# A decoder's first sublayer: triangular solve by halves of four tiles, two heads per operation

## The chip, the core and the metric

The kernel is one program on one core of a Trainium2 chip. It computes a four-layer decoder forward pass. The metric is the device time of the whole program in microseconds (us), median of several runs. Engines: TensorE (PE in the profile; PEld is its weight load), VectorE (DVE), ScalarE (ACT), GpSimd (POOL), SyncE (SP). PSUM, which PE writes, has eight banks of 512 fp32 columns on 128 partitions.

## What is computed

The change touches the first of eleven sublayers only, a gated delta rule attention with 6 heads, 32 key and 64 value channels, on 16 sequences of 64 tokens:

```
q = silu(conv(x @ Wq.T)); k = silu(conv(x @ Wk.T)); v = silu(conv(x @ Wv.T))
beta = sigmoid(x @ Wb.T);  g = -exp(A_log) * softplus(x @ Wa.T + dt_bias)
q, k = l2norm(q) * DK ** -0.5, l2norm(k)
def step(S, (qt, kt, vt, gt, bt)):          # over the 64 tokens
    S = S * exp(gt)
    v_new = vt - kt @ S
    S = S + bt * outer(kt, v_new)
    return S, qt @ S
o = scan(step); o = rmsnorm(o) * norm_w * silu(x @ Wg.T); x = x + o @ Wo.T
```

## The kernel before

The scan over tokens is written as a linear system for each head and sequence, solved by a blocked inverse. The 1024 tokens are 8 tiles (NT) of 128 partitions, and a tile holds two sequences of 64 (the two `halves` of the partitions, 0 to 63 and 64 to 127). So each step of the solve is, for one head, 8 tiles x 2 halves = 16 products of 64x64 by 64x64, one below the other on the diagonal of the PE array: `tile_position=(SEQ * half, SEQ * half)`, that is (0, 0) and (64, 64) in turn. An fp32 product is two matmul records in the trace, so a step of one head is a group of 32 records of 64 columns. The result of a head fills one PSUM bank, and one DVE or ACT operation of 128x512 takes it out.

The heads go in three pairs (a, b), and the solve stage runs from L2942 to L3353. `Fl` holds the levels of the system, made on POOL by `level` (L3140); `Rm` is the inverse built so far and `Tm` its transpose; `Wm` is a working square. For a pair and each of levels 1 to 4:

- `first` (L3009): PE forms W from `Fl` and `Tm`; ACT copies it out in `copy_w` (L3177);
- `second`: PE forms the update of the transpose (L3022, levels 1 to 3 only) and of the inverse (L3026); DVE subtracts them in `update` (`Tm` at L3254, `Rm` at L3255).

Then `solve` (L3034), copy (L3206), `pulled` (L3044), copy (L3209), `corrected` (L3052), `settled` on DVE (L3262), `outputs` (L3060), copy (L3215), squares (L3219, L3266). Between the groups of a pair PE does the front work for the heads of the next pair, n and m: `decays` (L2966), `keys` and `queries` (both L2974), `turn` (L2996). Its DVE steps are `decayed` (L3228), `pulls` (L3235), `reads` (L3241), `start` (L3245: identity minus level 0, the first inverse) and `copy_turned` (L3249). Each engine's queue is in the order in which it is written, and semaphores join them. `hold` (L1688) is filler work on PE. The stage behind (L3358 on) normalises and projects; its DVE queue begins at L3376.

The lists of buffers before the stage (L2865 to L2927) give each head squares of its own; heads 0 and 1 use banks 0 to 2 and 3 to 5 for the solve, and banks 6 and 7 serve the front work (3 and 4 for head 1).

## Time and profile before

| | us |
|---|---|
| median of 3 runs | 1345.42 (1344.11 to 1345.56) |
| the profiled execution, its own time | 1344.42 |
| span of its trace | 1342.7 |
| share of the span PE / DVE / ACT / POOL busy | 93% / 59% / 44% / 28% |
| mean granted PE clock | 0.993 of 2.4 GHz |

The profile is of one execution. The page gives busy times and groups over the whole program. The changed stage is under a tenth of it (about 84 to 198 us of the trace), so the readings below are from the time lines, windows and waits of that stretch. Matmuls overlap, so that "busy" of PE and the mean of one record say little; what a group costs is the distance from its start to the start of the next.

### The profile page before, as it was taken

Reading aid. Unit: us, or ns where it says so; the run is one execution under the profiler, and the core shown is the slowest. Engines: PE = TensorE matmul, PEld = TensorE weight load, DVE = VectorE, ACT = ScalarE, POOL = GpSimd, SP = SyncE. Lnnn points to the kernel's source line nnn. Section 1 sums busy time; section 2 is a strip of 40 time slices with the busy share of each in tenths; the row PEclk is TensorE's granted clock in tenths of the full one; section 3 lists DMA queues with packets and bytes.
Section 4 is the critical chain, followed back from the end, with each engine's and each line's share of the span. In section 5 each row is a group of like instructions: output and inputs, shape, how many; then the busy total and the mean of one; then the engine's idle time right before and its main releaser. Section 6 shows DMA issues by size and latency. Waiting matters only on the chain. (4 is left out here: it accounts for less than half of the span.)

```text
span 1342.7 us, 30256 instructions
## 1 busy us (share of the span) xinstructions
PE 1245.0 (93%) x12658; PEld 932.8 (69%) x12658; DVE 798.1 (59%) x1511; ACT 591.1 (44%) x1070; POOL 378.9 (28%) x323
## 2 busy tenths in 40 slices
PE   6999998989999999999999889999997888999988
PEld 3479994559977677788867667888774445676545
DVE  5764566863363764633358665888644775873762
ACT  3632334684554674433433431232532453662751
POOL 0164303046630000555520005544102043532100
PEclk9999999999999999999999999999998999999999
DMA  4000004046024001000075080000016421211000
GB/s 125 4 2 4 4 4 127 1 109 131 1 68 146 2 2 36 1 0 1 1 165 166 1 264 1 1 1 2 2 71 199 133 61 47 55 30 33 2 1 32
DMA packets 81047, 68.36 MB, mean 51 GB/s; under 512 B 24968, under 2 KB 76880, under 8 KB 80784
## 3 DMA queue, kind: packets, MB, share of 16 engines
q1 hardware_dynamic: 78096, 63.63, 16.8%
q8 instruction: 101, 1.65, 0.5%
q0 software_dynamic: 768, 2.10, 0.5%
q10 hardware_dynamic: 2048, 0.70, 0.2%
q14 instruction: 34, 0.28, 0.1%
HBM read 53.82 MB, written 8.39 MB: 46 GB/s over the span
## 5 line engine op out<-in xcount | busy, mean ns | idle before, releaser
L1955 PE MATMUL ps<-rounded 128*128 128x512 f32 x384 | 91.2, 393 | 2.0 <-POOL rounded L1988 1.0
L1688 PE MATMUL ps<-fixed 128*128 128x512 bf16 x361 | 89.6, 389 | 1.9 <-PEq L78 1.9
L1342 POOL TENSOR_TENSOR fixed<-fixed,cross 128x768 f32<-128x768 f32 x32 | 58.9, 1839 | 104.5 <-DVE cross L1291 104.5
L1955 PEld LDWEIGHTS ps<-rounded 128*128 128x128 f32 x384 | 70.9, 188 | 20.3 <-POOL rounded L1988 5.3
L1256 PE MATMUL ps<-rounded 128*128 128x256 f32 x576 | 76.8, 287 | 1.3 <-DVE cross L1287 1.3
L1256 PEld LDWEIGHTS ps<-rounded 128*128 128x128 f32 x576 | 70.7, 190 | 5.4 <-issue 3.2
L1988 POOL TENSOR_TENSOR rounded<-weights,rounded 128x256 fp32r<-128x256 f32 x32 | 23.6, 760 | 179.7 <-ACT rounded L2006 179.7
L1321 ACT COPY cross<-ps 128x256 f32<-128x256 f32 x32 | 11.9, 372 | 112.9 <-PE ps L1265 112.9
L1688 PEld LDWEIGHTS ps<-fixed 128*128 128x128 bf16 x361 | 34.7, 99 | 37.8 <-issue 6.9
L2095 DVE TENSOR_TENSOR work<-work,ps 128x512 f32<-128x512 f32 x32 | 22.0, 687 | 62.0 <-ACT work L2023 59.9
L1629 POOL TENSOR_TENSOR work<-weights,work 64x512 f32<-64x512 f32 x32 | 41.2, 1287 | 54.3 <-DMA work<-work 33.5
L1265 PE MATMUL ps<-fixed,work 128*128 128x256 f32 x192 | 49.3, 393 | 7.4 <-POOL fixed L1342 7.0
L1876 DVE SCALAR_TENSOR_TENSOR fixed<-ps,work,fixed 128x256 f32<-128x256 f32 x64 | 27.7, 479 | 46.7 <-PE ps L1779 46.7
L227 PE MATMUL ps<-fixed 128*128 128x128 f32 x160 | 30.3, 303 | 20.8 <-ACT fixed L212 16.2
L525 DVE TENSOR_REDUCE work<-ps 128x16 f32<-128x1024 f32 x32 | 39.2, 1224 | 17.5 <-PE ps L373 16.9
L201 ACT ACTIVATE fixed<-fixed 128x2 f32<-128x2 f32 x48 | 13.6, 293 | 80.7 <-DVE fixed L173 80.6
L1805 POOL TENSOR_TENSOR rounded<-work,rounded 128x512 fp32r<-128x512 f32 x32 | 41.1, 1300 | 27.7 <-ACT rounded L1836 27.2
L1779 PE MATMUL ps<-rounded 128*128 128x256 f32 x384 | 47.9, 284 | 0.0
L1779 PEld LDWEIGHTS ps<-rounded 128*128 128x128 f32 x384 | 47.2, 192 | 1.0 <-POOL rounded L1805 0.4
L1974 PEld LDWEIGHTS ps<-rounded 128*128 128x128 f32 x384 | 47.0, 192 | 0.5
L1974 PE MATMUL ps<-rounded 128*128 128x256 f32 x384 | 47.2, 283 | 0.0
L1752 PE MATMUL ps<-rounded 128*128 128x512 f32 x192 | 45.8, 393 | 1.4 <-POOL rounded L1792 1.4
(497 smaller groups left out, 3056.0 us busy)
## 6 DMA issues: line engine op xcount, KB each, us to landing
weights<-in_L_ffn_masksT SPq DMA_DIRECT2D x32, 256.0 KB, 6.1
weights<-in_L_ffn_fc_w SPq DMA_DIRECT2D x16, 256.0 KB
weights<-in_L_xattn_Wq SPq DMA_DIRECT2D x2, 2048.0 KB, 10.1
weights<-in_L_xattn_WoT SPq DMA_DIRECT2D x2, 2048.0 KB, 11.1
work<-work SPq DMA_DIRECT2D x64, 64.0 KB, 2.0
sorted_in<-work SPq DMA_DIRECT2D x1, 3072.0 KB, 15.3
work<-sorted_in SPq DMA_DIRECT2D x12, 256.0 KB, 2.9
sorted_out<-work SPq DMA_DIRECT2D x12, 256.0 KB, 2.1
```

What stands on the lines that cost most here:

```text
L227: last = nc.tensor.transpose(k.ps[:, banks[i % 2], (2 * c + jj) * P:(2 * c + jj + 1) * P], k.h[:, 2 * i + jj, c * P:(c + 1) * P], k.ident)
L525: nc.vector.tensor_reduce(mx[:, j % 2, gp, :], ps[:, 0:2, :].rearrange("p a (n t) -> p (a n) t", t=SEQ), AX.X, ALU.max).then_inc(s["maxed" ...
L1256: last = nc.tensor.matmul(seen[:, a, :], m[:, u % 2, c, a, :], of[:, c, part * D:(part + 1) * D], start=c == 0 and n == 0, stop=c == KC - ...
L1265: last = nc.tensor.matmul(ps[:, 2, 0:D], c1[:, v // 4, a, :], ro[:, v % 2, a, :], start=a == 0, stop=a == 2)
L1342: nc.gpsimd.tensor_tensor(ro[:, v % 2, :, :], ro[:, v % 2, :, :], sn, ALU.add).then_inc(s["roped"], 1)
L1629: last = nc.gpsimd.tensor_tensor(qb[64:128, 2 * (u % 2) + e, tok], cs[made, v % 2, :], turned_sn[made, v % 2, :], ALU.add)
L1688: k.nc.tensor.matmul(k.ps[:, bank, :], k.ident16, k.causal, start=True, stop=True)
L1752: last = nc.tensor.matmul(ps[:, 2 * m + half, :], a[:, q % 2, c, :], b[:, c, half * BANK:(half + 1) * BANK], start=c == 0 and part == 0, s ...
L1779: last = nc.tensor.matmul(ps[:, 4 + i, jj * D:(jj + 1) * D], a[:, (e - 1) % 2, c, j * P:(j + 1) * P], b[:, (e - 1) % 2, c, :], start=c == ...
L1805: nc.gpsimd.tensor_tensor(a_rest[:, e % 2, m, tok], act1[:, (4 * e + 2 * m + half) % 3, :], a_top[:, e % 2, m, tok], ALU.subtract).then_in ...
L1955: last = nc.tensor.matmul(ps[:, 2 * (n % 2) + i, :], a[:, q % 2, i, c, :], b[:, c, half * BANK:(half + 1) * BANK], start=c == 0 and part = ...
L1974: last = nc.tensor.matmul(ps[:, 4 + i, jj * D:(jj + 1) * D], a[:, (e - 1) % 2, c, j * P:(j + 1) * P], b[:, (e - 1) % 2, c, :], start=c == ...
```

## The change

A step of the solve is no longer "one head, eight tiles" but "one half q of four tiles, both heads of the pair" (e = 0 the even, e = 1 the odd head). The buffers of a pair become one tensor with a head axis (`Rp`, `Tp`, `Wp`, `Up`), and one ACT or DVE operation moves 2 heads x 4 tiles x 64 = 512 columns. The number of products, records and evacuations stays the same.

The inverses of the odd heads lie on the other rows: what belongs to the upper sequences sits on partitions 64 to 127 and the other way round (`inverse_rows`). `first`, `turned` (the transposes' update, split from `second`, with a semaphore XT of its own), `solve`, `pulled` and `corrected` go through `crosswise`: four products in a row stand at the four positions (0,0), (0,64), (64,64), (64,0) of the array (in the products from the inverse the second and the fourth are exchanged) and write two banks. `second` (the inverses' update) and `outputs` go through `straight`, with the diagonal positions as before, into bank 4 + q. Half q of the crosswise products uses banks 2q and 2q + 1.

The order on PE and DVE changes: `second` of half 1 of level l comes after `first` of half 0 of level l + 1, and on DVE the update of `Rm` of half 1 comes behind the front work of that level. PE's waits are now for both heads (both Fl semaphores; for level 1 also A and T1 of both). `start` of an odd head is two DVE operations on 64 partitions, from a square `odd_level` to the other rows. Six DMAs on the SP queue at the stage's start put the odd heads' values on the other rows (`crossed`), and the first `solve` waits for them. The output projections that are done early are those of tiles 4 to 7 in place of 2 to 5 (`part(1, c)` takes the place of `part(3, c)` behind).

```diff
-    gm, Wm = [square(spare) for _ in range(2)], [square(spare) for _ in range(2)]
+    gm, Wp = [square(spare) for _ in range(2)], spare.take(2, NT, SEQ)
+    Wm = [Wp[:, e] for e in range(2)]
...
-    used_gate = Region(w.gate.rearrange("p c s -> p (c s)"), 768)
-    dec, F, Um = ([square(k.work) for _ in range(2)] for _ in range(3))
+    dec, F = ([square(k.work) for _ in range(2)] for _ in range(2))
+    Up = k.work.take(2, NT, SEQ)
+    Um = [Up[:, e] for e in range(2)]
     A = [square(k.work) for _ in range(4)]
-    Rm = [square(hTs), square(hTs), square(used), square(used)]
-    Tm = [square(hTs), square(hTs), square(used), square(used_gate)]
+    Rp = [hTs.take(2, NT, SEQ), used.take(2, NT, SEQ)]
+    Tp = [hTs.take(2, NT, SEQ), k.spare.take(2, NT, SEQ)]
+    Rm, Tm = ([pair[:, e] for pair in pairs_of for e in range(2)] for pairs_of in (Rp, Tp))
+    crossed = k.spare.take(NH0 // 2, NT, DV0)
+    odd_level = square(k.spare)
...
+        def inverse_rows(e, half):
+
+            return (half + e) % 2
...
+        @block.sync
+        def _(sp):
+            odd = vt.rearrange("p j (g e d) -> p e g j d", e=2, d=DV0)[:, 1]
+            for half in range(2):
+                for g in range(NH0 // 2):
+                    sp.dma_start(crossed[halves[1 - half], g], odd[halves[half], g]).then_inc(s["swapped"], 16)
+            sp.wait_ge(s["swapped"], 16 * NH0)
...
+            def crosswise(q, stationary, moving, from_inverse):
+                for j in range(4 * q, 4 * q + 4):
+                    for half in range(2):
+                        for e in range(2):
+                            r = inverse_rows(e, half)
+                            rows, to = (r, half) if from_inverse else (half, r)
+                            last = nc.tensor.matmul(ps[halves[to], 2 * q + e, (j % 4) * SEQ:(j % 4 + 1) * SEQ], stationary(e, j)[halves[rows]],
+                                                    moving(e, j)[halves[rows]], start=True, stop=True, tile_position=(SEQ * rows, SEQ * to))
+                return last
+
+            def straight(q, stationary, moving, swapped):
+                for e in range(2):
+                    for j in range(4 * q, 4 * q + 4):
+                        for half in range(2):
+                            r = halves[inverse_rows(e, half) if swapped else half]
+                            at = 256 * e + (j % 4) * SEQ
+                            last = nc.tensor.matmul(ps[r, 4 + q, at:at + SEQ], stationary(e, j)[r], moving(e, j)[r],
+                                                    start=True, stop=True, tile_position=(r.start, r.start))
...
+            def first(p, l, q):
+                pe.wait_ge(s["Fl0"], 6 * p + l + 1)
+                pe.wait_ge(s["Fl1"], 6 * p + l + 1)
                 if l == 1:
-                    pe.wait_ge(s["A"], h + 1)
-                    pe.wait_ge(s["T1"], h + 1)
+                    pe.wait_ge(s["A"], 2 * p + 2)
+                    pe.wait_ge(s["T1"], 2 * p + 2)
                 else:
-                    pe.wait_ge(s["T"], nth(h, l - 1, 3))
...
+                    pe.wait_ge(s["T"], nth(p, l - 1, q, 3))
...
+                crosswise(q, lambda e, j: Fl[e][l][:, j, :], lambda e, j: Tp[p % 2][:, e, j, :], False).then_inc(s["W"], 1)
...
+            def turned(p, l, q):
+                pe.wait_ge(s["Ws"], nth(p, l, q, 4))
                 if l >= 2:
...
+                    pe.wait_ge(s["R"], nth(p, l - 1, q, 4))
+                crosswise(q, lambda e, j: Rp[p % 2][:, e, j, :], lambda e, j: Wp[:, e, j, :], True).then_inc(s["XT"], 1)
+
+            def second(p, l, q):
+                pe.wait_ge(s["Ws"], nth(p, l, q, 4))
+                if l >= 2:
+                    pe.wait_ge(s["R"], nth(p, l - 1, q, 4))
+                elif p:
+                    pe.wait_ge(s["Os"], 2 * p)
+                straight(q, lambda e, j: Wp[:, e, j, :], lambda e, j: Rp[p % 2][:, e, j, :], True).then_inc(s["XX"], 1)
...
+                n, m = 2 * p + 2, 2 * p + 3
+                more = p < 2
                 for l in range(1, 5):
-                    first(a, l)
-                    first(b, l)
-                    if more and l == 1:
-                        decays(n)
-                    if more and l == 2:
-                        queries(n)
-                    if more and l == 3:
-                        decays(m)
-                    if more and l == 4:
-                        keys(m)
-                    second(a, l)
-                    if more and l == 1:
-                        keys(n)
-                    if more and l == 3:
-                        turn(n)
-                    if more and l == 4:
-                        queries(m)
-                    second(b, l)
+                    first(p, l, 0)
+                    if l > 1:
+                        second(p, l - 1, 1)
+                    first(p, l, 1)
+                    if more:
+                        (decays, queries, turn, keys)[l - 1]((n, n, n, m)[l - 1])
+                    if l < 4:
+                        turned(p, l, 0)
+                    second(p, l, 0)
+                    if more and l != 2:
+                        (keys, None, decays, queries)[l - 1]((n, n, m, m)[l - 1])
+                    if l < 4:
+                        turned(p, l, 1)
...
-                nc.vector.tensor_tensor(Rm[h % 4], bc(eye, 1, NT), Rm[h % 4], ALU.subtract).then_inc(s["R1"], 1)
+                if h % 2:
+                    for half, own in enumerate(halves):
+                        last = nc.vector.tensor_tensor(Rm[h % 4][halves[1 - half]], bc(eye[own, :], 1, NT), odd_level[own], ALU.subtract)
+                    last.then_inc(s["R1"], 1)
+                else:
+                    nc.vector.tensor_tensor(Rm[h % 4], bc(eye, 1, NT), Rm[h % 4], ALU.subtract).then_inc(s["R1"], 1)
...
+            def update_turned(p, l, q):
+                dve.wait_ge(s["XT"], nth(p, l, q, 3))
+                own = half_of(Tp[p % 2], q)
+                nc.vector.tensor_tensor(own, own, solving(q), ALU.subtract).then_inc(s["T"], 1)
+
+            def update(p, l, q):
+                dve.wait_ge(s["XX"], nth(p, l, q, 4))
+                own = half_of(Rp[p % 2], q)
+                nc.vector.tensor_tensor(own, own, inverses(q), ALU.subtract).then_inc(s["R"], 1)
...
-                    update(a, l)
-                    update(b, l)
+                    if l < 4:
+                        update_turned(pair, l, 0)
+                    update(pair, l, 0)
+                    if l < 4:
+                        update_turned(pair, l, 1)
...
                         decayed(m)
                     if more and l == 4:
                         pulls(m)
+                    update(pair, l, 1)
+                    if more and l == 4:
                         reads(m)
                     if pair == 1 and l == 2:
```

`pulled`, `corrected` and `solve` are one call of `crosswise` each and `outputs` one of `straight`. ACT's `copy_w` and its other copies take `half_of(Wp, q)` from `solving(q)`, banks 2q and 2q + 1, columns 0 to 255; `settled` does the same on DVE.

## Rows read from the trace of the kernel before

**Rows 1.** The page: span, and busy time of each engine.

```profile
span 1342.7 us, 30256 instructions
PE 1245.0 (93%) x12658; PEld 932.8 (69%) x12658; DVE 798.1 (59%) x1511; ACT 591.1 (44%) x1070; POOL 378.9 (28%) x323
```

**Rows 2.** Windows of the three pairs (length, busy by engine, clock, DMA share, GB/s).

```profile
core 0: us, PE busy (x) PEld busy (x) DVE busy (x) ACT busy (x) POOL busy (x), PEclk, DMA share, GB/s
86.50:124.60 38.10, 37.62 (x1162) 35.64 (x1164) 19.15 (x27) 8.80 (x15) 24.41 (x23) 1.00 0.02 4
124.60:163.10 38.50, 37.70 (x1166) 35.48 (x1163) 19.24 (x30) 11.73 (x20) 17.18 (x17) 1.00 0.02 4
163.10:195.50 32.40, 32.00 (x988) 31.16 (x985) 16.89 (x28) 11.97 (x23) 1.43 (x2) 1.00 0.02 4
```

**Rows 3.** Waits, 86 to 197 us (who for whom: total, times, longest).

```profile
ACT fixed L3177 <- PE ps L3009: 56.9, 20, 8.6
DVE fixed L3254 <- PE ps L3026: 20.0, 11, 5.6
PE ps L2996 <- DVE fixed L3245: 0.4, 1, 0.4
```

**Rows 4.** Time line of PE, level 2 of pair 0 (start, length).

```profile
98.47 1.10 PE L3026 MATMUL ps<-fixed 64*64 64x64 f32 x32
99.41 1.10 PE L3022 MATMUL ps<-fixed 64*64 64x64 f32 x32
100.34 1.10 PE L3026 MATMUL ps<-fixed 64*64 64x64 f32 x32
101.28 1.44 PE L3009 MATMUL ps<-fixed,weights 64*64 64x64 f32 x38
```

**Rows 5.** Another sublayer's products at all four positions: time line, and durations (min/median/max).

```profile
449.64 1.10 PE L653 MATMUL ps<-weights,work 64*64 64x128 f32 x32
L653 PE MATMUL ps<-weights,work x256: 269/269/321, 449.6 to 500.3; 64*64 64x128 f32 x128
```

**Rows 6.** Groups from 74 to 200 us (busy, mean ns, idle before).

```profile
L3177 ACT COPY fixed<-ps 128x512 f32<-128x512 f32 x24 | 13.8, 585 | 56.9 <-PE ps L3009 56.9
L3254 DVE TENSOR_TENSOR fixed<-fixed,ps 128x512 f32<-128x512 f32 x12 | 8.2, 687 | 20.0 <-PE ps L3026 20.0
L3262 DVE TENSOR_TENSOR work<-fixed,ps 128x512 f32<-128x512 f32 x6 | 4.1, 687 | 5.2 <-PE ps L3052 5.2
```

**Rows 7.** Time line of DVE and of PE at the stage's head.

```profile
84.06 1.15 DVE L3245 TENSOR_TENSOR fixed<-weights,fixed 128x512 f32<-128x512 f32 x1
85.74 1.42 DVE L3249 COPY fixed<-ps 128x512 f32<-128x512 f32 x2
...
86.56 2.08 PE L3009 MATMUL ps<-fixed,weights 64*64 64x64 f32 x64
```

**Rows 8.** DVE and POOL in level 2 of pair 0 (time lines).

```profile
98.16 0.69 DVE L3235 TENSOR_TENSOR work<-work,ps 128x512 f32<-128x512 f32 x1 [1.09 <-POOL weights L3140]
...
92.30 7.83 POOL L3140 TENSOR_TENSOR weights<-work,weights 128x512 f32<-128x512 f32 x7
```

**Rows 9.** Tail of pair 0: time lines of PE, ACT and DVE.

```profile
115.45 2.10 PE L3034 MATMUL ps<-weights,fixed 64*64 64x64 f32 x64
119.79 1.15 PE L2996 MATMUL ps<-fixed,weights 64*64 64x64 f32 x32 [0.37 <-DVE weights L3245]
...
116.60 0.58 ACT L3206 COPY fixed<-ps 128x512 f32<-128x512 f32 x1 [4.70 <-PE ps L3034]
...
118.16 1.57 DVE L3245 TENSOR_TENSOR weights<-weights 128x512 f32<-128x512 f32 x1 [0.62 <-POOL weights L3140]
```

**Rows 10.** All `start` operations (durations min/median/max), and POOL beside the second pair's.

```profile
L3245 DVE TENSOR_TENSOR fixed<-weights,fixed x4: 885/1362/1582, 82.0 to 156.7; 128x512 f32<-128x512 f32 x4
...
117.03 8.91 POOL L3140 TENSOR_TENSOR weights<-work,weights 128x512 f32<-128x512 f32 x8 [13.39 <-DVE work L3235]
```

**Rows 11.** The stage's end and the next stage's first operation (time line).

```profile
197.75 0.25 DVE L3276 RECIPROCAL work<-work 128x16 f32<-128x16 f32 x1 [0.28 <-ACT work L3182]
...
198.68 0.42 DVE L3376 TENSOR_TENSOR work<-work 128x256 f32<-128x256 f32 x1 [0.67 <-PEq L78]
```

**Rows 12.** DMA issues of the page (KB each, us to landing), and a window behind the sublayer.

```profile
work<-work SPq DMA_DIRECT2D x64, 64.0 KB, 2.0
...
214.00:218.00 4.00, 3.04 (x11) 1.50 (x12) 1.84 (x3) 0.59 (x1) 4.00 (x5) 0.70 0.38 90
```

203 lines of the change are left out of this document (87 added, 116 removed).

## The prediction

> **What bounds the kernel now.** The page shows PE busy for 93% of the span and DVE for 59% [rows 1], but the change lies in one stage, so I read that stage alone. The windows of the three pairs come first: PE is busy for 37.62 of 38.10 us, 37.70 of 38.50 and 32.00 of 32.40, DVE for about half of each, ACT for a quarter to a third, at a granted clock of 1.00 [rows 2]. The waits say the same from the other side: ACT idles 56.9 us for `first`, DVE 20.0 us for the inverse's update, and the longest kind of wait of PE there is 0.4 us [rows 3]. So PE sets the length of this stage, by the groups it is given. What a group costs is read from the time line: the starts at 98.47, 99.41, 100.34 and 101.28 are 0.93 to 0.94 us apart, for 32 records of 64 columns at the two diagonal positions [rows 4], 29 ns a record.
>
> **What four positions are worth.** The one stretch of this trace that uses all four positions is L653 in another sublayer. Its 32 records have twice the columns (128), and yet the run of them lasts 1.10 us with 0.27 us for the last one, so that they start (1.10 - 0.27) / 31 = 27 ns apart [rows 5]. Twice the columns in the same time means that four records run abreast there, against two in the solve. For a crosswise group of 64 columns the bounds are therefore: below, half of L653's 32 x 27 = 0.86 us, 0.43; above, 0.93, if only the diagonal pair ever overlaps at this width. Half of today's group is 0.47. I take 0.52, near the low end because rows 5 show the overlap itself, and 0.05 above the half for PE's waits on two or three semaphores per group, which come twice as often per unit of time.
>
> Here a rule of the Trainium skill speaks against the change. "TensorE: Matmul & The Clock Gate" (section "Wait — 56ns, not 53.3ns?") says that start-to-start never drops below about 25 ns however few the columns. Rows 4 and 5 with 29 and 27 ns do not contradict it. By it a crosswise group would take 32 x 25 = 0.80 us, an estimate from the page; its result stands beside rival B.
>
> **The sum, part by part.** A pair has 30 groups: 8 `first`, 6 transposes' updates, 8 inverses' updates, and 2 each of `solve`, `pulled`, `corrected`, `outputs`. 8 + 6 + 6 = 20 become crosswise, 10 stay diagonal. *Removed from PE:* 3 x 20 x (0.93 - 0.52) = 24.6 us. Operations of ACT and DVE keep their number and width (128x512: 0.585 and 0.687 us [rows 6]).
>
> PE was never waiting, and now it will. I laid the four queues beside each other in the new order with durations from the rows. The latencies: `solve` of two heads starts at 115.45, its first group's last record 31 x 28.5 ns = 0.88 later, the copy at 116.60, so 0.27 from the last record to ACT; `start` ends at 118.16 + 1.57 = 119.73 and PE's `turn` begins at 119.79, 0.06 from DVE to PE [rows 9]. *Given back:*
> - Head. The first `first` began at 86.56 and needed only head 0; now it needs both copies, which end at 85.74 + 1.42 = 87.16 [rows 7], and `start` of head 1 is a second operation of about 1.1 (its one is 1.15 [rows 7]) in front of them. 88.3 instead of 86.56: 1.7 us.
> - Pair 0, level 2. `pulls` starts at 98.16, released by POOL, whose queue is unbroken from 92.30 [rows 8] and gets no faster. The inverse's update of half 1 now stands behind `pulls` on DVE: done at 98.16 + 0.6 + 0.69, PE goes on at about 99.5. By then its groups (six crosswise, three diagonal, decays, keys, queries from 88.3) end at 97.8. Hole: 1.6 us. Queued behind the waiting PE instruction are `first` of level 3 and with it POOL's levels for the next pair.
> - `turn` of heads 2 and 4 comes earlier on PE (level 3, ahead of the updates) than `start` delivers it: 0.5 each, 1.1 us.
> - Tails. A half's round is 0.50 + 0.27 + 0.585 + 0.05 = 1.4 us by ACT and 1.5 by DVE, and the two halves fill only 1.04 of it. Empty: 0.45 before the second `solve`, 0.35 before the second `pulled`, 0.5 before `outputs`: 1.3 per pair, 3.9 us.
> - `start` of heads 3 and 5 as two operations. One took 1.57 with POOL busy all through [rows 9, 10]; two at 1.4, and DVE reaches them earlier: `turn` waits some 0.9 us longer in each of two pairs, 1.8 us. Bounds: two at the least value of 0.885 [rows 10] give 0.8 less in each pair, two at 1.57 0.2 more.
> - Level 1 of pairs 1 and 2. W's copy stands on ACT behind `outputs`' copy and two squares, and PE now has 1.04 instead of 1.87 us of `first` to cover that: 0.2 + 1.0 = 1.2 us.
> - Pair 2. `scaled` and `gated` (two operations each) are in front of the updates on DVE, in levels with 3.9 us of PE work instead of 5.6: 1.1 us.
>
> Together 12.4; of today's 1.7 us without PE in the three windows [rows 2] about half is in places where PE now arrives later than its operand, 0.9 less. Net 11.5 given back, so 24.6 - 11.5 = 13.1 us.
>
> The Trainium skill has a rule for the `start` item ("SBUF — State Buffer", section "SBUF: two separate sides"): a VectorE operation with two SBUF inputs and a GpSimd operation take one port pair in turn, for the whole instruction. The trace agrees: the six `start` operations spread from 0.885 to 1.582, the long ones beside an unbroken POOL. Waiting out a rest of a POOL operation twice instead of once is what 1.4 each stands for; taken as two full turns the item would be 0.5 us worse, which changes nothing else.
>
> **At nothing:** the six DMAs. They bring 128 KB each from SBUF to SBUF, are issued at the stage's start on an otherwise idle queue with a DMA share of 0.02 [rows 2], and are first needed some 30 us later; pieces of 64 KB land in 2.0 us [rows 12]. Without that cover the first `solve` would wait 10 to 25 us. Also at nothing: other tiles for the early projections (same groups, same place), and the diagonal order inside `straight`. The stage end is the same chain of squares, root and reciprocal (197.75, next stage at 198.68 [rows 11]), so that what the stage gains the program gains: no transfer is waited for in it.
>
> **Result.** The profiled execution's own 1344.42 - 13.1 = 1331.3; against the median of the runs, 1.0 higher, 1345.42 - 13.1 = **1332.3 us**. Ends of the sum: groups of 0.47 (27.6 removed) and `start` operations without POOL's hindrance give 17.5, 1327.9; groups of 0.60 give about 11, 1334.5.
>
> **Rivals.**
> - *B, records don't start closer than they do anywhere now.* For: no two rows here show less than 27 ns, with two instructions to issue per record. Against: rows 5 are explained by column count alone. Groups of 0.86 remove 60 x 0.07 = 4.2, and because PE comes later the holes shrink to about 1.8: 1343.0. (By the page's 25 ns the same layout gives 7.8 - 2.2 = 5.6, 1339.8.)
> - *C, positions that share rows or columns take turns.* Then no two neighbours of a crosswise group overlap, while the diagonal pair did. Place: every crosswise group; price: a record alone takes 2 x 29 = 58 ns, so 1.87 us a group, 60 x 0.94 = 56 us less the holes: about 1400. It decides from a group of about 0.97 us, where what is left of the holes (1.7 at the head and little else) plus 60 x 0.04 passes 0.2%. Against it stand rows 5; only half the columns is new.
> - *D, the chain of halves binds more than laid out.* DVE is in order: R of half 1 waits behind up to two front operations, and each of the six levels with front work may lose another 0.69 us: 4.1 more, 1336.4. For: a level with front work gives DVE some six operations of 0.687, 4.1 us and more beside POOL, against PE's new 5.8 (four groups of 0.52, two of 0.93, two of front work). Against: T, which `first` needs, goes ahead of them.
> - *The clock.* PE with holes might be granted less: behind this sublayer a window with PE busy 3.04 of 4.00 us has 0.70 [rows 12]. The new holes are 1.6 us at most between dense groups, as the present ones of the head, at 1.00. I give it 2%.
>
> **How the numbers follow.** Forecast 0.60 (own range 1327.5 to 1335.5), D 0.12, B 0.18, C and a fall of the clock 0.10. The range from 1327.5 to 1342.0 holds the forecast, D and the faster half of B, about 0.8. A measurement of this kernel tells about 0.2%, 2.7 us, from no change. Faster by more: forecast, D and two thirds of B, 0.83. Within: the rest of B and a C near its deciding point, 0.09. Slower: 0.08.
>
> **What would show it.** On the time line of PE a crosswise group (32 records of 64x64) lasts about 0.5 us from start to start and a straight one 0.93; PE's idle time in the stage is 13 us instead of 2, with `turn`, `solve` and `outputs` among those that wait, for DVE and ACT; the first `first` begins 1.7 us later; `pulls` of head 2 still begins near 98.2; the pairs take about 33.5, 33 and 30 us instead of 38.0, 38.5 and 34.9 (from each first `first` to the next, the last to the stage's end). If crosswise groups take 0.8 or more, the step "four abreast at 64 columns" is wrong; if they take 0.5 and the stage gains under 10, the holes are.

## The result: half of the expected gain

The changed kernel takes 1341.28 us (median of 20 runs, 1335.48 to 1351.11) against 1346.07 for the kernel before, measured beside it. The ratio is 0.9954, with a 95% interval from 0.9937 to 0.9972: 6.2 us faster (the medians are 4.8 us apart). Predicted were 13.1 us less. A second group of runs gave a ratio of 0.9990 only (0.9970 to 1.0009, e14_after_again); what of that is the granted clock is told below. Medians in this text are of all runs of a group and ratios of the fast ones alone, so that one run of e5_no_swap (1753.83 us at a granted clock of 0.65) and two of the kernel before are in no ratio. The profiled execution took 1337.37 us (span 1335.6) against 1344.42, but a profiled execution scatters by some microseconds in the other sublayers, so the comparison below is made in the stage itself: from VectorE's first operation in it to the end of the last reciprocal. That was 123.5 us before (74.55 to 198.00, [rows 11]) and is 117.5 now (73.84 to 191.31), 6.0 us less; in the second profile of the change it is 116.6.

"PE" is TensorE, "PEld" its weight loads, DVE VectorE, ACT ScalarE, POOL GpSimd. The page of after, and windows of the three pairs, each from its first `first` (columns: length, busy time of each engine, granted clock, DMA share, GB/s). They answer to rows 1 and 2:

```profile
span 1335.6 us, 30284 instructions
PE 1221.7 (91%) x12658; PEld 907.3 (68%) x12658; DVE 802.5 (60%) x1514; ACT 591.1 (44%) x1070; POOL 380.5 (28%) x323
...
87.92:122.24 34.32, 29.30 (x1163) 26.90 (x1166) 19.58 (x27) 8.62 (x15) 25.12 (x23) 1.00 0.02 5
122.24:158.41 36.17, 31.32 (x1168) 28.10 (x1168) 20.78 (x31) 11.65 (x20) 17.24 (x16) 0.95 0.02 4
158.41:187.73 29.32, 23.66 (x981) 21.93 (x978) 16.88 (x28) 11.31 (x21) 0.00 (x0) 1.00 0.02 5
```

PE's busy time fell by 23.3 us in the whole program, close to the 24.6 of the prediction. So the work did go away. But now PE is idle for 5.0, 4.9 and 5.7 us in the windows, where it was idle for 0.4 to 0.8. The time line of PE shows the groups themselves (start, length, shape, records; in brackets the idle time before). It answers to rows 4:

```profile
92.34 0.69 PE L3038 MATMUL ps<-fixed 64*64 64x64 f32 x32
92.86 0.65 PE L3038 MATMUL ps<-fixed,weights 64*64 64x64 f32 x32
93.32 1.03 PE L3048 MATMUL ps<-fixed 64*64 64x64 f32 x29
...
94.83 0.85 PE L3005 MATMUL ps<-work 32*64 32x64 f32 x21
96.07 0.56 PE L3005 MATMUL ps<-work 32*64 32x64 f32 x11 [0.40 <-issue]
96.56 0.69 PE L3038 MATMUL ps<-fixed 64*64 64x64 f32 x32
97.08 1.11 PE L3048 MATMUL ps<-fixed 64*64 64x64 f32 x32
99.20 0.51 PE L3038 MATMUL ps<-fixed 64*64 64x64 f32 x19 [1.01 <-DVE fixed L3296]
```

Crosswise groups (L3038) start 0.52 us before their successor here, which is also the median of all 60 when pauses are left out; the shortest take 0.47. Four records do run abreast, 15 ns from one start to the next. Straight groups (L3048) take 0.87 to 0.93. The last line is the hole behind `pulls` that was forecast. The surprise is the line of 96.07: a group of `queries` (L3005) breaks off after 21 of its 32 records and goes on 0.4 us later. No instruction inside a group waits for a semaphore, and the profile knows no releaser either ("issue"). The waits of the weight loads in the stage show how much of that there is (who for whom: total us, times, longest):

```profile
PEld ps L3038 <- issue: 8.8, 18, 1.2
PEld ps L3038 <- ACT fixed L3207: 3.2, 3, 1.5
PEld ps L3048 <- issue: 2.0, 3, 1.5
PEld ps L3028 <- DVE fixed L3279: 1.8, 1, 1.8
PEld ps L3028 <- DVE weights L3279: 1.6, 1, 1.6
PEld ps L3028 <- issue: 0.9, 1, 0.9
```

In the kernel before, "issue" stands for 2.8 us of such waits in the same stretch, the longest 0.3.

**Where the breaks are.** I numbered PE's instructions (loads, products and the waits for semaphores between them) in the order of the trace. The breaks inside groups end at 96.07, 107.53, 115.14, 130.11, 134.08, 138.15, 141.98, 145.64, 165.47, 169.51, 173.36, 177.99, 181.71 and 185.52, and all of them end at an instruction whose number is 193 or 194 modulo 256. The transfers of the same stretch name the thing:

```profile
DMA packets 28, 0.44 MB, mean 4 GB/s; under 512 B 0, under 2 KB 0, under 8 KB 0
## 3 DMA queue, kind: packets, MB, share of 16 engines
q8 instruction: 26, 0.43, 1.8%
```

Queue q8 brings 26 packets of 16 KB of instructions, one for each 256 instructions of PE (16384 / 256 = 64 bytes each; DVE, ACT and POOL together execute some 250 instructions there, no page's worth). I call such a packet a page of instructions. An example from the packets' times: PE goes on at 165.47, the next packet starts at 166.61 and ends at 167.93; at 167.97 PE stops, and it goes on at 169.51, 1.58 us after the packet's end. All 14 breaks look like this: PE goes on 1.26 to 1.60 us after the end of the last packet, and the next packet starts 1.1 to 2.1 us after that. This fits a page that is sent for when PE enters the page before it; the three parts (until the packet starts, the packet, until PE goes on) add up to the distance. From one such restart to the next it takes 4.04, 3.85, 4.63, 3.72 and 3.81 us (165.47 to 185.52). So a series of pages comes no faster than some 3.7 to 3.9 us each, even if PE works through them in less. Crosswise groups (64 instructions in 0.47 us) would work through one in 1.9. After a wait a page can lie ready: the fastest 256 instructions of the stage took 2.3 us (from 160.9, behind a pause of 1.6).

This is theory S, supply of instructions (the texts written before the runs call its pauses "stalls without a releaser"). Its rival Q was that the holes and orders which the prediction listed are larger than it said and nothing else binds. The runs were chosen to tell them apart.

### The profile page after: what moved, and what is told of

It reads as the page before. It is cut to its first block and busy times, and to the rows that moved or that the text cites. A ratio compares the mean times of both kernels' runs of the same rounds, so it can differ in the third digit from the quotient of the medians.

```text
span 1335.6 us, 30284 instructions
## 1 busy us (share of the span) xinstructions
PE 1221.7 (91%) x12658; PEld 907.3 (68%) x12658; DVE 802.5 (60%) x1514; ACT 591.1 (44%) x1070; POOL 380.5 (28%) x323
```

## The experiments

One table first, because single comparisons of whole runs are no better than 3 us here. "Stage" is the length in the profiled execution. "At page ends" and "elsewhere" are sums over PE's stretch from the first `first` to the last product of `outputs` (107.95 us before, 99.81 after): of the distances between starts of PE's records over 0.12 us, each less 30 ns. "At page ends" are those that end where the instruction's number modulo 256 is 187 to 195, "elsewhere" the others. The latter is not comparable where most records are 128 columns wide and start further apart anyway, and holds some 0.12 us at each seam between unlike groups.

```
kernel                  stage    at page ends   elsewhere   ratio to before (95%)
before                  123.5     0.1            9.6        1
after                   117.5     9.6           16.7        0.9954 (0.9937-0.9972)
e14_after_again         116.6     9.3           16.0        0.9990 (0.9970-1.0009)
e5_no_swap              121.0     0.2            6.5        1.0012 (0.9985-1.0039)
e1_two_abreast          119.4     6.1           12.6        0.9954 (0.9931-0.9977)
e2_half_columns         117.3    11.0           13.5        0.9959 (0.9931-0.9987)
e4_pages_shifted        118.3     9.1           18.1        one run
e7_wide_no_swap         119.5     0.8            7.6        0.9961 (0.9936-0.9985)
e6_wide_straight        109.7     6.0             -         0.9892 (0.9845-0.9939)
e13_all_wide            106.6     0.2             -         0.9887 (0.9846-0.9928)
e12_one_start           115.5    13.2           11.5        one run
e16_pulls_behind        118.6    11.6           15.0        one run
e3_shared_load          116.7     9.8           16.5        0.9939 (0.9915-0.9963)
e8_dve_turn             118.2    10.9           17.0        0.9968 (0.9942-0.9995)
e11_turn_reordered      115.2    12.4           13.6        0.9946 (0.9927-0.9964)
e10_turn_and_load       112.3    14.1           14.8        0.9944 (0.9924-0.9964)
e15_turn_and_load_2     109.6    10.0           15.9        0.9911 (0.9877-0.9946)
```

One thing more moves these stages. In after and in e14, and in e1 to e4, e6, e8, e9, e11 to e13 and e16, the profile has one or more stretches in the stage with a granted clock of 0.50, mostly of 3.4 us; in before, in both kernels without the swap (e5, e7), in e10 and in e15 it has none. A stretch of 3.4 us costs up to 1.7 us.

### The limit by itself

**e9_probe.**

```diff
+            for i in range(1024):
+                a, c = i // 2 % 2, i % 2
+                nc.tensor.matmul(ps[halves[c], 1 + a, 0:8], k.ident16[halves[a], 0:SEQ], k.causal[halves[a], 0:8],
+                                 start=True, stop=True, tile_position=(SEQ * a, SEQ * c))
             pe.wait_ge(s["ocopied"], 4)
```

> After, with 1024 products of 8 columns (2048 instructions, 8 pages) at the end of the stage's work on TensorE, spread over the four positions; their results go nowhere. The crosswise products showed 15 ns from one start to the next in bursts, which would be 1024 x 15 = 15 us for these. Theory S: 8 pages at 3.9 us, 31 us, in bursts of one page with a stall after each 256 instructions. If TensorE had a steady limit for each product in place of a page limit, the starts would be evenly spaced.

PE's time line, start of the series:

```profile
189.82 0.34 PE L3149 MATMUL ps<-fixed 64*64 64x8 bf16 x20
191.31 1.36 PE L3149 MATMUL ps<-fixed 64*64 64x8 bf16 x128 [1.15 <-issue]
195.04 1.88 PE L3149 MATMUL ps<-fixed 64*64 64x8 bf16 x128 [2.37 <-issue]
198.49 1.87 PE L3149 MATMUL ps<-fixed 64*64 64x8 bf16 x128 [1.58 <-issue]
202.22 1.88 PE L3149 MATMUL ps<-fixed 64*64 64x8 bf16 x128 [1.85 <-issue]
```

The series took 29.0 us (189.41 to 218.40; 31 were expected), and it comes in blocks of exactly 128 products, 256 instructions. Blocks start 3.45 to 4.00 us apart, 3.73 on average, though PE needs 1.36 us for the first whole one and 1.88 for the others (the granted clock is 0.50 from 192.1 on, the lower level of 1.2 GHz). Each block starts 1.34 to 1.56 us after the end of a packet on q8, as the breaks in the kernel do. There is no evenly spread limit per product. Theory S is shown for this limit; the stage of e5 below shows that it costs PE next to nothing (0.2 us) where 256 instructions keep it busy for 3.7 us.

**e4_pages_shifted.**

```diff
+            for _ in range(40):
+                nc.tensor.matmul(ps[0:32, 5, 0:8], k.ident16[:, 0:32], k.causal[:, 0:8], start=True, stop=True)
             for h in range(2):
                 turn(h)
```

> After, with 40 products of 8 columns (80 instructions) in the head of the stage, where TensorE waits for the first inverses anyway. Theory S: the stalls inside groups stay at the same place of the page (the instruction's number modulo 256, counted with the added ones) and so move to instructions 80 earlier in the program; the time stays within 2 us of after. Theory Q: they stay at the same products.

The time is that of after (1337.49 against its profiled 1337.37). I numbered the stage's own records, without the 40. In after, pauses at page ends stand before records 1650, 1776, 1903, 2028, 2788, 2914 and 3040; here before 1611, 1737, 1863, 1989, 2748, 2874 and 3000, 39 or 40 records (80 instructions) earlier. The large pauses for operands stay: records 588, 716, 1200, 1296, 1428, 2264, 2328, 2360 and 2584 in both. Moving code without changing it moves one kind of pause and not the other.

**e2_half_columns.**

```diff
-                            last = nc.tensor.matmul(ps[r, 4 + q, at:at + SEQ], stationary(e, j)[r], moving(e, j)[r],
+                            last = nc.tensor.matmul(ps[r, 4 + q, at:at + cols], stationary(e, j)[r], moving(e, j)[r, 0:cols],
```

> The straight products (the inverse's updates and the outputs, 28 of 30 groups of 32 records) compute only 32 of their 64 columns; the rest of the columns is left out, so the values are wrong. The number of instructions is that of after. TensorE's work falls by 28 groups x about 0.46 us = 12.9 us. Theory Q: most of that is gained, 8 to 12 us (1329 to 1333). Theory S: the pages arrive no faster, so 0 to 3 us are gained (1338 to 1341) and the stalls without a releaser grow from 12.9 us to over 20.

No gain (stage 117.3), but this run tells nothing for either theory, and the stalls did not grow to over 20 us as S had it (12.7). A straight group of 32 records with 32 columns still takes 0.9 us: at two positions a record costs 28 ns with half the columns as with all. PE's busy time did not fall (86.8 us in the stretch in which after has 84.3), so the premise, 12.9 us of work less, was wrong.

### What swap, halves and page limit are worth

**e5_no_swap.**

```diff
         def inverse_rows(e, half):
-            return (half + e) % 2
+            return half
@@ start of odd heads
-                    for half, own in enumerate(halves):
-                        last = nc.vector.tensor_tensor(Rm[h % 4][halves[1 - half]], bc(eye[own, :], 1, NT), odd_level[own], ALU.subtract)
-                    last.then_inc(s["R1"], 1)
+                    nc.vector.tensor_tensor(Rm[h % 4], bc(eye, 1, NT), odd_level, ALU.subtract).then_inc(s["R1"], 1)
```

> The change without its crosswise part: halves of four tiles, both heads of a pair per operation and the banks by half stay, but all products lie on the diagonal positions (groups of 0.93 us), the odd heads' inverses stay on their own rows, their start is one operation, and the six transfers are gone. TensorE's work is that of before. Theory S: the pages keep up with products at 0.93 us a group, so this is before plus the holes that halves make: 1345 to 1351 us, stalls without a releaser under 5 us. If it comes out near 1341 as after does, the swap and the four abreast are worth nothing at all and the halves alone made the gain. Theory Q: 1345 plus some 10 us of holes, 1355.

The edit also orders the crosswise products head by head and reads the odd heads' values from their own rows. The six transfers, which the text above calls gone, are still issued (6 of 128 KB, landing in 3.2 us) and waited for, as in after.

1347.61 us, ratio 1.0012 (0.9985 to 1.0039). By whole runs the halves alone bring nothing. By the stage they bring 2.5 of the 6.0 us (121.0 against 123.5; one profile each, which scatter by about 1), because PE waits less outside page ends (6.5 us for 9.6). By it the swap brings the other 3.5. PE, from the first `first` to the last output product, and its waits without a releaser:

```profile
86.90:192.50 105.60, 104.16 (x3300) 100.06 (x3296) 53.61 (x86) 32.03 (x56) 43.23 (x40) 1.00 0.02 4
...
PEld ps L3038 <- issue: 3.0, 9, 1.0
```

With groups of 0.93 us only 0.2 us are lost at page ends. Four groups of 64 instructions take 3.7 us there, so that PE itself leaves the pages nearly all of the time they need.

**e1_two_abreast.**

```diff
-                for j in range(4 * q, 4 * q + 4):
-                    for half in range(2):
-                        for e in range(2):
+                for e in range(2):
+                    for j in range(4 * q, 4 * q + 4):
+                        for half in range(2):
```

> The change as it is, except that the crosswise products go head by head, so that successive ones use two positions of the array (as the straight ones do) and not four; the same instructions, the same operands. Theory S (instruction supply: TensorE gets its instructions in pages of 256 and a new page costs about 3.9 us, so that the time won by four abreast is taken back by stalls at page boundaries): this kernel has the holes of the change but hardly any page stalls. The stage of after is 6.0 us shorter than before = 24.6 won, less 12.9 us of stalls without a releaser, less holes of about 6; so this one should be before plus about 6: near 1352 us, stalls without a releaser under 4 us. Theory Q (the holes and orders that the prediction listed are simply larger, 19 us in all, nothing else binds): before plus 19, near 1365 us, and the stalls without a releaser stay.

1342.7 us: neither. One reason is that the edit does only part of what it says. Where one head's positions follow the other's, records of both overlap, so that a crosswise group is shorter than 0.93: from start to start, pauses left out, the median is 0.68 us, against 0.52 in after. PE's stretch of 101.7 us less its pauses is 83.0 us, against 99.8 - 26.3 = 73.5 in after. That is 9.5 us of work more, and the stage is only 1.9 us longer (119.4). Pauses at page ends fall from 9.6 to 6.1 and the others from 16.7 to 12.6. Four fifths of what four abreast saves over this order is given back as waiting, nearly half of that at page ends.

**e6_wide_straight** and **e7_wide_no_swap** (the same edit in after and in e5_no_swap).

```diff
-                    for j in range(4 * q, 4 * q + 4):
+                    for j in range(4 * q, 4 * q + 4, 2):
@@
-                            last = nc.tensor.matmul(ps[r, 4 + q, at:at + SEQ], stationary(e, j)[r], moving(e, j)[r],
+                            last = nc.tensor.matmul(ps[r, 4 + q, at:at + 2 * SEQ], stationary(e, j)[r], moving(e, slice(j, j + 2))[r],
```

> After, with each two straight products of 64 columns as one of 128 columns through the first one's stationary tile: TensorE streams the same columns, with half the instructions (30 groups x 32 = 960 fewer, 3.75 pages); the second tile's values are wrong. Theory S: up to 3.75 x 3.9 = 14.6 us less, as far as the holes let it: 8 to 14 us under after (1327 to 1333), and the stalls without a releaser fall below 6 us. Theory Q: TensorE's work and all waits are the same, so the time is that of after (1341).

> The wide straight products (960 instructions fewer) on the kernel without the swap. Theory S: there TensorE's own work binds, not the pages, so this is within 2 us of the kernel without the swap. If it is 8 us or more below it, the supply of instructions bound that kernel too (and so the kernel before).

With the swap the stage falls by 7.8 us (117.5 to 109.7), without it by 1.5 (121.0 to 119.5). "The same columns" was not quite the same work: a wide straight group takes about 0.80 us in place of 0.93, 30 x 0.13 = 3.9 us. Of the 7.8 us, 3.9 is thus PE's own work, and pauses at page ends fell by 3.6 (9.6 to 6.0). The direction is S's; the median of 1330.66 lies in the 1327 to 1333 that I expected, but only half of the stage's gain is page supply, since a page that is not passed is only worth what PE had waited for it. Whole runs show the contrast less well than the stages: e7 has 1341.41 us and a ratio of 0.9961, 0.0051 (7 us) under e5, where within 2 us were expected; e6 is 0.0062 (8 us) under after. Of e7's 7 us the stage shows 1.5 and about 2 go with the clock (median 0.992, e5's 0.990); the rest is not explained. In e7 the wide groups save 3.2 us of PE's work, of which the stage gets 1.5: 0.6 went to page ends and 1.1 to other waits.

**e13_all_wide** does it to the crosswise products as well.

> Both the straight and the crosswise products in pairs of tiles through the first one's stationary tile (128 columns each, the second tile's values wrong): TensorE streams after's columns with 60 groups x 32 = 1920 instructions fewer, 7.5 pages. If the missing part of the gain is all page supply, the stage comes down to what the prediction had worked out, some 111 us (1332.3 for the whole), or to the run with wide straight products (109.7), and the stalls without a releaser are under 4 us between 84 and 190 us. If the holes that the prediction listed are larger than it said, they show here alone: a stage over 113 us with few stalls without a releaser.

Pauses at page ends vanish (0.2 us), and the stage comes down to 106.6 us, ratio 0.9887. The window of PE's stretch and its waits now:

```profile
86.85:176.10 89.25, 77.68 (x1854) 67.82 (x1856) 56.51 (x87) 31.57 (x56) 42.80 (x39) 0.98 0.01 3
...
PEld ps L3038 <- issue: 5.6, 11, 1.1
PEld ps L3048 <- DVE work L3303: 2.4, 3, 0.9
PEld ps L3038 <- ACT fixed L3207: 2.3, 2, 1.7
PEld ps L3028 <- DVE fixed L3279: 2.0, 1, 2.0
PEld ps L3038 <- DVE fixed L3296: 1.7, 3, 0.9
```

PE is idle for 89.25 - 77.68 = 11.6 us. With the head (1.7 later than before) that is what the prediction's list of holes should have come to: it said 11.5 in all, here it is 11.6 - 1.6 (before's idle time in that stretch) + 1.7 = 11.7. So no hidden holes are left that the list lacked; that the sums meet to 0.2 us is partly luck, since shorter groups make PE wait longer for the same operands. The stage is below the 110.4 that the prediction implied (123.5 - 13.1) because PE's groups are shorter again (straight ones 0.80; a crosswise one 0.42 from its first record to its last, in place of 0.47). The "issue" left here (5.6 us, under 4 in all were expected) is no page limit: PE's pauses over 0.35 us stand at the first record of a group or, twice, inside `decays`.

### Two holes taken out one at a time

**e12_one_start** leaves out the second half of `start` of heads 3 and 5 (`enumerate(halves if h == 1 else halves[:1])`).

> After, with only the first half of the odd heads' start for heads 3 and 5 (the second half of their inverses is left out, so the values are wrong): one operation of about 1.5 us fewer in front of the turns of heads 3 and 5. The prediction priced the second operation at 1.8 us in all. Theory Q: the stage is 2 to 3 us shorter than after's 117.5. Theory S: the wait in front of the turn falls by 1.5 us each time, but a page that would have arrived in it is now waited for: under 1 us in all.

**e16_pulls_behind** moves `pulls` of heads 2 and 4 behind the update of the second half.

> After, with only the update of the second half ahead of the next pair's pulls at the first level. The prediction priced the hole behind the pulls in pair 0 at 1.6 us. If holes and pages add up, the stage is 1 to 2 us shorter than after's 117.5; if the pages fill the hole anyway, it is within 0.8 us of it.

Both took pauses away elsewhere: 16.7 to 11.5 and 16.7 to 15.0 us. Both lost more at page ends: 9.6 to 13.2 and 9.6 to 11.6. The stages are 115.5 and 118.6 against 117.5 and, in a second profile of after, 116.6. So of the 5.2 us taken out of e12's holes 3.6 came back at page ends and 2.0 at most were gained, the least that theory Q asked for and twice the most that S did; e16 gained nothing, and at 1.1 us over after it met neither text. A profiled stage scatters by about 1 us, so these two runs decide nothing alone; what they show is the move of pauses from holes to page ends. e16 also had two stretches of 3.4 us at half the clock in the stage (from 87.7 and from 118.5), after one.

### Fewer instructions as a remedy

**e3_shared_load.** Keys and queries of heads 2 to 5 through one load, 256 instructions fewer.

```diff
+                        last = nc.tensor.matmul(ps[own, front_banks(h)[side], at:at + P], qk[rows, 2 + n, tokens(j, half)],
+                                                qk[rows, n::2, tokens(j, half)], start=True, stop=True,
+                                                tile_position=(32 * (h % 3), SEQ * half))
```

> Keys and queries of heads 2 to 5 have the same stationary tile; here one load serves 128 columns (query and key side by side) in place of two loads and 64 columns each. TensorE streams as many columns as before, but 4 x 64 = 256 instructions fewer are issued, one page. Theory S: one page less, 3 to 4 us less than after (about 1337.5). Theory Q: the same work in the same slots, 0 (1341), or up to 1 us more because the product with the keys comes a slot later.

The stage is 0.8 us shorter, 1340.70 us, ratio 0.9939: in the right direction, too little to be told from after, and less than the 3 to 4 us. The pauses at page ends are unchanged (9.8), only one page fewer is passed. Its stage has two stretches of 3.4 us at half the clock (from 87.3 and from 111.2) where after's has one.

**e8_dve_turn.** The first inverses are turned by VectorE.

```diff
-                nc.vector.tensor_copy(flat(Tm[h % 4]), ps[:, front_banks(h)[1], :]).then_inc(s["T1"], 1)
+                nc.vector.transpose(flat(Tm[h % 4]), flat(odd_level if h % 2 else Rm[h % 4])).then_inc(s["T1"], 1)
```

> After, with the first inverses turned by VectorE in blocks of 32x32 (the level-0 factor is zero outside them) in place of TensorE's turn and VectorE's copy out of the bank: 6 x 64 = 384 instructions of TensorE fewer (1.5 pages), 6 groups of 0.93 us of its work gone, one VectorE operation more per odd head. Theory S: 1.5 x 3.9 = 5.9 us less, 4 to 7 with what VectorE gives back: 1334 to 1337. Theory Q: the two waits for the odd heads' start (3.6 us) and part of the 5.6 us of work, so a similar 3 to 8 us; the stalls without a releaser stay at 15 us there, and fall under theory S only where fewer pages are passed.

A miss: 1341.88 us, stage 118.2. With no turns to do PE was idle in the head for 6.5 us (82.68 to 89.19), and the window from there reads:

```profile
84.50:94.70 10.20, 5.51 (x124) 4.50 (x125) 5.16 (x6) 1.77 (x3) 10.20 (x10) 0.50 0.01 2
```

The granted clock was 0.50 for 10.2 us, and the first crosswise groups took about 0.85 us in place of 0.47. So this run says nothing on what fewer instructions are worth.

**e11_turn_reordered** and **e10_turn_and_load** add 18 filler products in the head, and turn the odd heads first and copy their inverses to the other rows behind that; e10 has the shared load too.

> The same without the shared load of keys and queries (384 instructions fewer, not 640). Theory S: one page, 2 to 4 us, more than the version with both. Against the run with VectorE's turn alone (1341.9, whose first products ran at the lower clock and whose stage was 118.2 us) it has the fillers and the earlier turn of the odd heads: 3 to 5 us less, 1337 to 1339.

> A version meant to gain by fewer instructions on TensorE: one load for keys and queries of heads 2 to 5 (256 fewer), the first inverses turned by VectorE (384 fewer), the odd heads' inverse turned first and copied to the other rows behind that, and 18 fillers in the head so that the clock does not fall. 640 instructions fewer (36 of them back as fillers) are 2.4 pages, 9 us by theory S, of which the wide straight run suggests some two thirds arrive: 5 to 7 us less than after, 1334 to 1336. Theory Q: the turns and their waits gone, 3.6 us of waits and up to 5.6 us of work: about the same, so this run is for the version and not for the rivals.

**e15_turn_and_load_2** is e10 with `pulls` behind the update and those copies behind the settled halves, and it ran beside **e14_after_again**.

```diff
-                        pulls(n)
@@
                     update(pair, l, 1)
+                    if more and l == 1:
+                        pulls(n)
@@
                 settled(pair, 0)
                 settled(pair, 1)
+                if more:
+                    move_rows(m)
```

> The version with the shared load and VectorE's turn, and two orders on VectorE changed: the inverse's update of the second half ahead of the next pair's pulls (behind which it stood 3.2 us for GpSimd in pair 0), and the copies of the odd heads' inverses to the other rows behind the settled pairs (for which the outputs waited 3.2 us in all). Up to 5 us of holes; where a page is late there anyway less: 2 to 4 us under the version before it, stage about 109 us, 3 to 8 us under after.

> The change as it is, on the same chip as the others of this group, so that versions are compared with it and not only with the kernel before: 1341 us, 6 us under before.

e10 and e11 gave 1338.72 and 1340.49 us, ratios 0.9944 and 0.9946, 1.3 us at most under after's and both slower than expected, though e10's stage is 5.2 us shorter. e15 gave 1334.27 us, ratio 0.9911 (0.9877 to 0.9946), where the change beside it gave 1344.94 and 0.9990 (0.9970 to 1.0009). It beats both kernels: 12 us under before, its stage 109.6 us (109 were expected), and 5 us under the change at a like clock (worked out below). PE in it:

```profile
86.30:179.60 93.30, 78.77 (x3041) 70.66 (x3040) 62.04 (x91) 31.73 (x56) 43.66 (x39) 1.00 0.02 4
```

The two ratios of the change, 0.9954 and 0.9990, are 5 us apart. Each run lists its mean granted clock, and over the runs of one kernel 0.01 of it goes with about 10 us (7 to 14 in all groups but e7's, which has 4). The change's runs at 0.991 to 0.993 in the second group took 1337 to 1339 us and those at 0.984 to 0.988 took 1343 to 1350; before's took 1343 to 1347 at 0.991 to 0.993, and 1353.7 and 1352.6 at 0.984 and 0.987. Brought to 0.990 at 10 us for each 0.01, an estimate, the medians are 1341.2 and 1341.0 us for the change's two groups, 1347.0 to 1347.9 for before's four, and 1335.9 for e15. At a like clock the change is thus worth 6 to 7 us both times. But 9 of its 12 runs in the second group were at the low end, and 2 of before's 17. Part of this the change may bring about itself, as the stretches at half the clock in the stage suggest; how much of it the sublayers behind do stays open.

## Why the prediction was wrong

The crosswise groups and the holes hold, point by point; the failed step is the one between them, that every microsecond taken from PE's groups which no listed operand claims back leaves the stage. The sum had no term for the supply of PE's instructions, and the runs showed 9.5 us of pauses at page ends. All numbers for the stage, in us; work is PE's stretch less its pauses:

```
                                            predicted     measured
PE's work (60 crosswise groups)               -24.6       73.5 - 98.2              = -24.7
head: first `first`                            +1.7       (87.92-73.84)-(86.57-74.55) = +2.1
waits for operands behind it                   +9.8       16.7 - 9.6               =  +7.1
pauses at page ends                               0       9.6 - 0.1                =  +9.5
behind the last product                           0       3.6 - 3.5                =  +0.1
sum                                           -13.1                                   -5.9
stage                                                     117.5 - 123.5            =  -6.0
```

That the work agrees to 0.1 is closer than its parts do: it holds the 3.4 us at half the clock (from 153.6), which cost up to 1.7, and straight groups that came out shorter (0.87 us, median, for 0.93). That the measured 1341.28 us lie inside the range that was stated (1327.5 to 1342.0) is luck: its upper end was there for rivals B and D, and neither came.

- **Four abreast at 64 columns.** Right: the median from start to start is 0.52 us with pauses left out, as taken, and the shortest groups, at 0.47, are at half of the old one. Rivals B and C fall with it. The Trainium skill ("TensorE: Matmul & The Clock Gate", section "Wait — 56ns, not 53.3ns?") puts the least distance of starts at about 25 ns; the trace shows 15 ns when neighbours lie at four positions. At one position the 40 products of e4 do start 25 ns apart, so that figure holds there.
- **The head.** 2.1 us for 1.7.
- **The hole behind `pulls`.** Predicted near 98.2 on before's clock; it stands at 97.77 where the stage began 0.7 earlier, and PE waits 1.2 us for 1.6:

```profile
97.77 0.69 DVE L3265 TENSOR_TENSOR work<-work,ps 128x512 f32<-128x512 f32 x1 [3.20 <-POOL weights L3170]
98.37 0.68 DVE L3296 TENSOR_TENSOR fixed<-fixed,ps 128x512 f32<-128x512 f32 x1
```

- **`turn` of heads 2 and 4.** 0.76 and 0.29 us, 1.05 for 1.1. **Tails.** Some 0.8 to 1.3 a pair, for 1.3.
- **`start` of heads 3 and 5.** The pauses before `turn` are 1.7 and 1.9 us where they were 0.6 each, so 2.4 for 1.8. The operations of 64 partitions take as long as one of 128 did [rows 10]; two at 1.5, not at 1.4 (the bound for two at 1.57 was also off: they are 2 x 0.17 = 0.34 us above two at 1.4, not 0.2):

```profile
L3279 DVE TENSOR_TENSOR fixed<-weights,work x4: 876/1476/1486, 83.5 to 151.4; 64x512 f32<-64x512 f32 x4
L3279 DVE TENSOR_TENSOR weights<-weights,work x2: 1486/1519/1552, 114.6 to 116.1; 64x512 f32<-64x512 f32 x2
```

- **Level 1 of pairs 1 and 2.** 1.1 and 1.6 us (124.75 and 160.93) for 1.2 together: mis-sized. **`scaled` and `gated`.** No pause of their own is to be seen; in that pair page ends took 5.0 us (165.47 to 185.52) and may have covered them.
- **The six DMAs** land in 3.1 us and no wait for them shows, and the stage's end is the same chain (191.05, next stage at 191.90). Right. **Rival D** asked for 4.1 us of waits more than the list; there are 2.7 fewer.
- **The clock.** Named as a rival at 2% because all new holes seemed short. In a small way it came: there was one stretch of 3.4 us (in the second profile of the change too, at 153.7), which begins 0.6 us after the end of the pause of 1.9 us before the `turn` of head 5:

```profile
153.60:157.00 3.40, 3.40 (x98) 3.27 (x96) 2.06 (x3) 0.00 (x0) 3.40 (x4) 0.51 0.03 5
```

- **Pairs.** 34.3, 36.2 and 32.9 us for 33.5, 33 and 30. The text said that if crosswise groups take 0.5 and the stage gains under 10, the holes are wrong. They were not (7.1 us for 9.8, and 2.1 for 1.7 at the head); a limit was missing that the sum had no term for.

**Could it have been seen before?** Yes, as a bound. In before's trace PE's stretch from 86.57 to 194.51 has 3296 records and as many loads, with the waits 26 pages, and takes 107.9 us, 4.15 us a page; no two of its packets of instructions start less than 3.59 us apart. The forecast asked for 107.9 - 24.6 + 9.8 = 93.1 us, 3.58 a page on average, and for single levels at 5.8 us for two pages. At the probe's 3.73 us the 26 pages take 97.0, an estimate of the least, and after's stretch took 99.8. That is no proof of a limit, but it is a rate of which the trace had no row, and it should have been a rival with a price from 0 to (4.15 - 3.58) x 26 = 15 us.

The Trainium skill bears on this ("Runtime: NRT & Kernel Launch", section "Instruction fetch mechanics"): pages of 256 instructions are fetched one ahead by a queue of each engine, and the cost of passing a boundary is mostly hidden, because dispatch is slower than the fetch. The trace agrees on the pages and on the queue. It does not agree that the cost is hidden here: 9.6 us in 15 pauses in after, where PE works through 256 instructions in less than the 3.7 us that the next ones take.

## What to carry to other kernels

An engine's busy time is not its only bound: count its instructions in a stage, waits included, divide by 256, and if a faster form leaves less than about 3.7 us for each 256 (3.73 in the probe, 3.7 to 3.9 mostly in this kernel), price it at that. Where products are made of many small ones, fewer and wider instructions (one load for two uses, a turn on another engine) may then be worth more than more of them abreast (e15 got 5 us out of it at a like clock; e3, with one page fewer, nothing that could be measured), and a hole that is closed may only move to the next page end. Look for it as pauses inside a group, released by nothing, at equal distances in the count of instructions.

## What the runs showed of the hardware

- Instructions for PE come in packets of 16 KB for 256 instructions. In a series that waits for nothing else, 256 of them take 3.73 us on average (3.45 to 4.00, e9_probe, nearly all of it at 0.50 of the clock; 3.72 and 3.81 from restart to restart in after at 1.00). The packet itself is on its way for 0.9 to 1.4 us of that; it starts 1.1 to 2.1 us after PE entered the page before, and PE goes on 1.26 to 1.60 us after its end (14 breaks of after).
- Products of 64x64 start 15 ns apart at four positions, 28 to 29 ns at two, whether 64 or 32 columns are streamed (e2). With 128 columns it is about 50 ns at two positions (e6).
- Records overlap across the seam of two heads or groups where their positions differ: in e1 a crosswise group takes 0.68 us (median) though neighbours inside a head use only two positions; with the diagonal pair alone it takes 0.93 (e5).
- An operation of VectorE on 64 partitions beside a busy POOL takes 1.5 us, no less than one on 128 [rows 10].
- The granted clock fell to 0.50 for 10.2 us from 84.5 on, while PE was idle in the head of e8 (82.68 to 89.19), and for 30.7 us during the probe, in which PE was busy for 12.4 of 25.9 us.
